# Softplus of delta summed by VectorE in two banks instead of by four TensorE products

## The chip, the core and the metric

One core of a Trainium2 chip runs the whole program. The metric is the device time of one execution in microseconds. The engines are TensorE (PE: matmuls; PEld: its weight loads), VectorE (DVE), ScalarE (ACT), GpSimd (POOL) and SyncE (SP), which issues DMAs; each runs its own instructions in order and they meet at semaphores.

## The reference

For 32 sequences of 256 steps and 128 features, a layer norm and a selective state space layer are added to x, and then a layer norm and a feed-forward layer with 8 routed experts (two of them weighed in per step) and a shared one. What the change touches is the step size delta:

```
g = u @ W_gate.T                       # u: silu of the causal convolution
delta_lo, b, c = g[:64], g[64:80], g[80:96]
delta = softplus(delta_lo @ W_delta.T + delta_bias)
A = -exp(A_log)
h = exp(A * delta) * h + (delta * u) * b        # per step, 16 states per channel
y = sum over states of h * c, + D * u
```

All of it is fp32. Softplus is computed as max(z, 0) + log(1 + e), e = exp(-|z|), with a correction: w = 1 + e is rounded, so e - (w - 1) is what the rounding lost, and delta = relu(z) + log(w) + (e - (w - 1)).

## The kernel before

The kernel is a software pipeline over sequences, written out by hand: `steps` (line 286) runs `body(k, on)` for k = -3 to 34 on each engine, and `on(lag)` asks whether sequence k + lag exists. One body, one period, works on several sequences at once: sequence k in its scans, k+1 in delta and its gate, k+2 in layer norm, convolution, u, g and z, k-1 in the projection, the second layer norm and the router, k-2 in the feed-forward layer. The order of the lines in each engine's body is the order of that engine's queue; nothing else decides it.

Per sequence there are 8 groups of states. For group q, ScalarE writes the decays exp(A delta) into one of two halves of a four-bank PSUM tile (`decays`, line 444, four instructions of 255 columns), POOL multiplies delta*u by b (`inject_group`, line 377), VectorE scans them (`scan`, line 643, 1024 columns), POOL multiplies the states by c (`read_group`, line 386), and TensorE sums over states (`sum_states`, line 847). POOL thus has 16 operations of 1024 columns in a period. `decays` of a group waits for the scan two groups before it.

The feed-forward layer has 14 chunks of features in 7 pairs: `gates` (860) and `ups` (869) on TensorE, silu on ScalarE, the product on VectorE (`gated_up`, 653), the expert weights spread by TensorE (`spread_comb`, 882) and multiplied in by VectorE (`weigh`, 661), and `down` (890). Pairs 0 to 3 are made at the end of the period before and at its start, pairs 4 to 6 in the middle.

Three PSUM banks of 512 columns serve everything else in turn. `z_ps` (line 164) lies in bank 2, `delta_ps` (158) in bank 0. The way of z and delta before: TensorE makes z for sequence k+2 (line 1030). ScalarE reads it four times in halves (its bias differs by half): |z + bias| into z_e (560), relu(z + bias) into z_relu (563). After decays 7 it makes exp (580), after decays 0 of the next sequence w = 1 + e in z_w (591) and w - 1 in z_kept (593). In the next body TensorE adds z_e, minus z_kept and z_relu into `delta_ps` with an identity and a negative identity as weights (963 to 965, behind `sum_states(k, 0)`), ScalarE takes the logarithm of z_w (508), and TensorE adds it (991, behind `sum_states(k, 2)`). VectorE multiplies delta by u (780), ScalarE copies delta (536), and SP spreads both over the partitions with 8 DMAs (330).

ScalarE changes its activation table five times a period: silu (456), exp (483), logarithm (504), silu (520), exp (548).

## Time and profile before

| | |
|---|---|
| median of three runs | 1453.29 us (1452.8 to 1456.53) |
| the profiled execution | 1453.74 us |
| its span, first to last instruction | 1451.6 us |
| instructions | 26176 |
| mean granted TensorE clock | 0.961 of 2.4 GHz |
| busy: DVE, ACT | 1042.5 us (72%), 1080.1 us (74%) |

The span is a start of some 150 us in which the pipeline fills, 28 alike periods, and an end of some 130 us in which it empties. The granted clock is full in nearly all of the middle. An engine's busy share says how much it does, not whether anybody waits for it; the chain of waits says what was late, and an engine's timeline gives in brackets how long it idled before a group and who released it.

### The profile page before, as it was taken

The page shows a single profiled execution, that of the slowest core. Times are in us where ns is not written, and L with a number is a line of the kernel's source. Part 1 is how long each engine was busy: PE and PEld are TensorE (multiplying, and loading weights), DVE is VectorE, ACT ScalarE, POOL GpSimd, SP SyncE. Part 2 cuts the span into 40 slices and gives each one's busy share as a digit, 9 for nine tenths or more (in the row PEclk, how much of TensorE's full clock was granted, in tenths as well). Part 3 has the DMA queues.
Part 4 walks back from the last instruction along what each step waited for, and adds up shares of the span by engine and source line. Part 5 has one row for each costly group of instructions (what it writes and reads, how often), then busy time and mean ns, then how long its engine had stood idle before and what let it go on. Part 6 is the DMA issues. An engine that isn't in the chain of part 4 may idle for free.

```text
span 1451.6 us, 26176 instructions
## 1 busy us (share of the span) xinstructions
PE 1273.9 (88%) x9203; PEld 950.7 (65%) x9203; DVE 1042.5 (72%) x1664; ACT 1080.1 (74%) x2219; POOL 1219.0 (84%) x568
## 2 busy tenths in 40 slices
PE   3455999999999999999999999999999999998888
PEld 2223766777667667776676677766766777665677
DVE  2245778877777788777777887777778877776753
ACT  3777778777877787778777877787778777876642
POOL 3299898898889988988899889888998898899920
PEclk8667999999999999999999999999999999999989
DMA  3433322333333223333332233333322333233000
GB/s 102 103 89 84 92 67 69 95 96 92 74 86 95 65 70 96 96 93 75 84 94 66 70 96 96 92 74 85 95 65 69 96 97 92 69 83 89 7 5 8
DMA packets 71486, 115.08 MB, mean 79 GB/s; under 512 B 8174, under 2 KB 30396, under 8 KB 71356
## 3 DMA queue, kind: packets, MB, share of 16 engines
q1 hardware_dynamic: 67180, 110.71, 30.2%
q10 hardware_dynamic: 4176, 2.70, 0.6%
q8 instruction: 73, 1.20, 0.3%
q14 instruction: 57, 0.47, 0.1%
HBM read 41.04 MB, written 5.24 MB: 32 GB/s over the span
## 4 chain that ended last, share of the span: by engine, by line
PE 34%; DVE 22%; ACT 17%; issue 16%; POOL 1%; DVEq 0%; SPq 0%; DMA 0%; ACTq 0%; POOLq 0%
DVE state L648 11%; PE work_ps L864 10%; PE work_ps L873 10%; ACT decay_ps L451 6%; DVE features L666 5%; PE acc_ps L898 4%; ACT L483 3%; ACT L504 3%; PE acc_ps L856 3%; ACT L548 3%; PE work_ps L1081 2%; PE work_ps L997 2%; PE work_ps L927 2%; ACT u L526 2%; DVE features L658 2%
## 5 line engine op out<-in xcount | busy, mean ns | idle before, releaser
L393 POOL TENSOR_TENSOR read<-state,bc 128x1024 f32<-128x1024 f32 x256 | 605.6, 2379 | 93.0 <-DVE state L648 87.6
L384 POOL TENSOR_TENSOR inject<-rep,bc 128x1024 f32<-128x1024 f32 x256 | 604.4, 2385 | 52.2 <-DMA rep<-dd 52.2
L648 DVE TENSOR_TENSOR_SCAN state<-decay_ps,inject 128x1024 f32<-128x1024 f32 x256 | 580.9, 2280 | 48.3 <-ACT decay_ps L451 29.5
L451 ACT ACTIVATE decay_ps<-rep,neg_a 128x255 f32<-128x255 f32 x1024 | 423.5, 462 | 14.6 <-DVE state L648 5.5
L442 ACT ACTIVATE g_silu<-work_ps 128x512 f32<-128x512 f32 x224 | 133.9, 598 | 204.3 <-PE work_ps L864 204.0
L658 DVE TENSOR_TENSOR features<-g_silu,work_ps 128x512 f32<-128x512 f32 x224 | 151.6, 678 | 147.5 <-PE work_ps L873 107.5
L898 PE MATMUL acc_ps<-ffn_down,features 128*128 128x128 f32 (+1 forms) x1792 | 252.5, 284 | 0.0
L898 PEld LDWEIGHTS acc_ps<-ffn_down,features 128*128 128x128 f32 (+1 forms) x1792 | 217.2, 191 | 30.1 <-issue 12.3
L864 PE MATMUL work_ps<-xn2T_part,ffn_gate 128*128 128x256 f32 x1344 | 210.9, 294 | 2.5 <-ACT combT L499 1.8
L873 PE MATMUL work_ps<-xn2T_part,ffn_up 128*128 128x256 f32 x1344 | 207.7, 291 | 1.4 <-ACT dd L536 1.4
L856 PE MATMUL acc_ps<-read,sum_sel 128*32 128x256 f32 x2048 | 168.3, 401 | 37.8 <-POOL read L393 37.6
L873 PEld LDWEIGHTS work_ps<-xn2T_part,ffn_up 128*128 128x128 f32 x1344 | 180.5, 195 | 27.4 <-ACT dd L536 13.6
L864 PEld LDWEIGHTS work_ps<-xn2T_part,ffn_gate 128*128 128x128 f32 x1344 | 180.6, 196 | 17.4 <-issue 13.1
L666 DVE TENSOR_TENSOR features<-features,work_ps 128x512 f32<-128x512 f32 (+1 forms) x192 | 113.9, 630 | 18.1 <-PE work_ps L885 18.1
L979 PE MATMUL work_ps<-xnT_part,wconv 128*128 128x256 f32 x768 | 103.2, 292 | 26.7 <-DVE xnT_part L769 26.7
L979 PEld LDWEIGHTS work_ps<-xnT_part,wconv 128*128 128x128 f32 x768 | 96.5, 194 | 37.2 <-DVE xnT_part L769 36.4
L856 PEld LDWEIGHTS acc_ps<-read,sum_sel 128*32 128x32 f32 x2048 | 40.8, 109 | 110.0 <-POOL read L393 49.2
L885 PE MATMUL work_ps<-combT,csel 40*128 40x256 f32 x352 | 87.4, 334 | 2.0 <-DVE features L658 2.0
L474 ACT ACTIVATE gate<-work_ps 128x512 f32<-128x512 f32 x32 | 19.1, 596 | 66.8 <-PE work_ps L927 66.8
L885 PEld LDWEIGHTS work_ps<-combT,csel 40*128 40x128 f32 x352 | 53.4, 185 | 20.4 <-DVE features L658 2.8
L927 PE MATMUL work_ps<-xnT_part,wo 128*128 128x256 f32 x192 | 32.3, 305 | 34.4 <-DVE features L658 30.7
L780 DVE TENSOR_TENSOR dd<-work_ps,u 128x512 f32<-128x512 f32 x32 | 22.1, 691 | 48.9 <-PE work_ps L991 48.9
(134 smaller groups left out, 1398.5 us busy)
## 6 DMA issues: line engine op xcount, KB each, us to landing
rep<-dd SPq DMA_DIRECT2D x256, 256.0 KB, 4.8
bc<-bc_rows SPq DMA_DIRECT2D x64, 512.0 KB, 4.8
x_in<-in_L_attn_x_dram SPq DMA_DIRECT2D x32, 128.0 KB, 2.2
out_dram<-result SPq DMA_DIRECT2D x32, 128.0 KB, 1.8
bc_rows<-g_sb SPq DMA_DIRECT2D x32, 32.0 KB
state<-in_L_ffn_w_gate_dram ACTq DMA_DIRECT2D x1, 704.0 KB, 4.4
read<-in_L_ffn_w_up_dram ACTq DMA_DIRECT2D x1, 704.0 KB, 5.9
ffn_down<-in_L_ffn_w_down_dram ACTq DMA_DIRECT2D x1, 704.0 KB, 7.1
```

The costliest lines, as they stand in the source:

```text
L384: pool.tensor_tensor(inject[:, at % RI], du_all, b_all, ALU.mult).then_inc(inject_done, 1)
L393: pool.tensor_tensor(read[:, at % RR], state[:, at % RS], c_all, ALU.mult).then_inc(read_done, 1)
L451: last = act.activation(decay_ps[:, at % 2, j, 1:T], rep[n % 2][:, half * JB + j, 0, 1:T], ACT.Exp, scale=neg_a[:, col:col + 1])
L648: dve.tensor_tensor_scan(state[:, at % RS].rearrange("p j t -> p (j t)"), decay_ps[:, at % 2].rearrange("p j t -> p (j t)"), inject[:, at ...
L658: dve.tensor_tensor(features[:, 2 * p:2 * p + 2, :].rearrange("p c t -> p (c t)"), g_silu[p % 2][:], banks[UP_BANK[p]][:], ALU.mult).then_ ...
L666: dve.tensor_tensor(to, to, banks[COMB_BANK[i]][:, 0:len(chunks) * T], ALU.mult).then_inc(hc_done, 1)
L856: last = pe.matmul(y_ps[j * CB:(j + 1) * CB, :], sum_sel[:], read[:, at % RR, j, :], start=False, stop=(g == SG - 1), skip_group_check=True)
L864: last = pe.matmul(banks[GATE_BANK[p]][:, side * T:(side + 1) * T], ffn_gate[w][:, chunk * P:(chunk + 1) * P], xn2T_parts[n % 2][d][:], st ...
L873: last = pe.matmul(banks[UP_BANK[p]][:, side * T:(side + 1) * T], ffn_up[w][:, chunk * P:(chunk + 1) * P], xn2T_parts[n % 2][d][:], start= ...
L885: last = pe.matmul(banks[COMB_BANK[i]][:, at * T:(at + 1) * T], csel[:, (chunk - NSH) * P:(chunk - NSH + 1) * P], combT[:], start=True, st ...
L898: last = pe.matmul(down_ps[:, j * DIM:(j + 1) * DIM], features[0:r, chunk, j * P:(j + 1) * P], ffn_down[0:r, chunk, :], start=fresh and j ...
L979: last = pe.matmul(conv_ps[:, half * T:(half + 1) * T], wconv[w][:, half, tap, :], xnT_parts[d][:, tap:tap + T], start=(w + d + tap == 0), ...
```

## The change

The bias of delta becomes a row of W_delta and a row of ones under g, so that the product of line 1030 brings it in (97 rows in place of 64, with 32 rows of zeros against b and c); it is loaded straight into that row. ScalarE then makes |z|, e and w in one pass each, one after the other between decays 5 and 6, and no relu and no w - 1. VectorE makes, in the bank of z, s = max(z, 0) + e, and then z_less = (w - 1) - s in SBUF, both between the fourth and the fifth weighing, ahead of scan 6. In the next body ScalarE writes log(w) straight into the bank of delta, and VectorE subtracts z_less in place, just before it multiplies by u. The four groups of products are gone, and the negative identity, z_kept and z_relu with them. Waits are added or renamed to suit.

```diff
-        wdelta = sb("wdelta", [RANK, HALVES, P])
+
+        wdelta = sb("wdelta", [GATES + 1, HALVES, P])
...
-        g_sb = sb("g_sb", [GATES, T])
+        g_sb = sb("g_sb", [GATES + 1, T])
         z_e = sb("z_e", [P, HALVES, T])
         z_w = sb("z_w", [P, HALVES, T])
-        z_kept = sb("z_kept", [P, HALVES, T])
-        z_relu = sb("z_relu", [P, HALVES, T])
+        z_less = sb("z_less", [P, HALVES, T])
...
+            (wdelta[GATES:GATES + 1, :, :], delta_bias.rearrange("(o c p) -> o c p", o=1, p=P)),
...
                     sp.wait_ge(dd_done, n + 1)
+                    sp.wait_ge(du_done, n + 1)
                     sp.wait_ge(decay_done, count(GROUPS * k))
...
                     act.wait_ge(z_one_done, n + 1)
-                    act.activation(z_w[:], z_w[:], ACT.Ln).then_inc(z_log_done, 1)
+                    act.wait_ge(du_done, n)
+                    if on(-1):
+                        act.wait_ge(x1_done, k)
+                    act.activation(delta_ps, z_w[:], ACT.Ln).then_inc(z_log_done, 1)
...
                     decays(k, 5)
-                    decays(k, 6)
                 if on(3) or on(-1):
                     act.wait_ge(ln_small, 2 * (k + 4))
                     act.activation(rstd[:], log_var[:], ACT.Exp, scale=-0.5).then_inc(ln_rstd, 1)
                 if on(2):
                     n = k + 2
                     act.wait_ge(z_mm, n + 1)
-                    act.wait_ge(delta_mm, n)
-                    for half in range(HALVES):
-                        last = act.activation(z_e[:, half, :], z_ps[:, half, :], ACT.Abs, bias=delta_b[:, half:half + 1])
-                    last.then_inc(z_abs_done, 1)
-                    for half in range(HALVES):
-                        last = act.activation(z_relu[:, half, :], z_ps[:, half, :], ACT.Relu,
-                                              bias=delta_b[:, half:half + 1])
-                    last.then_inc(z_relu_done, 1)
-                if on(0):
+                    act.wait_ge(z_sum_done, n)
+                    act.activation(z_e[:], z_ps, ACT.Abs).then_inc(z_abs_done, 1)
+                    act.wait_ge(z_abs_done, n + 1)
+                    act.activation(z_e[:], z_e[:], ACT.Exp, scale=-1.0).then_inc(z_exp_done, 1)
+                    act.wait_ge(z_exp_done, n + 1)
+                    act.wait_ge(z_log_done, n)
+                    act.wait_ge(z_less_done, n)
+                    act.activation(z_w[:], z_e[:], ACT.Identity, bias=1.0).then_inc(z_one_done, 1)
+                if on(0):
+                    decays(k, 6)
                     decays(k, 7)
...
-                if on(2):
-                    n = k + 2
-                    act.wait_ge(z_abs_done, n + 1)
-                    act.activation(z_e[:], z_e[:], ACT.Exp, scale=-1.0).then_inc(z_exp_done, 1)
                 if on(1):
                     decays(k + 1, 0)
...
-                if on(2):
-                    n = k + 2
-                    act.wait_ge(z_exp_done, n + 1)
-                    act.activation(z_w[:], z_e[:], ACT.Identity, bias=1.0).then_inc(z_one_done, 1)
-                    act.wait_ge(z_one_done, n + 1)
-                    act.activation(z_kept[:], z_w[:], ACT.Identity, bias=neg_one[:, 0:1]).then_inc(z_kept_done, 1)
                 if on(1):
                     decays(k + 1, 1)
...
-            dve.memset(neg_one[:], -1.0).then_inc(prep, 1)
+            dve.memset(wdelta[RANK:GATES, :, :], 0.0).then_inc(prep, 1)
+            dve.memset(g_sb[GATES:GATES + 1, :], 1.0).then_inc(prep, 1)
...
-                    dve.wait_ge(delta_mm, n + 1)
+                    dve.wait_ge(z_log_done, n + 1)
+                    dve.wait_ge(z_less_done, n + 1)
+                    dve.tensor_tensor(delta_ps, delta_ps, z_less[:], ALU.subtract).then_inc(delta_done, 1)
+                    dve.wait_ge(delta_done, n + 1)
                     for half in range(HALVES):
                         dve.wait_ge(rep_in[half], 16 * JB * n)
                     dve.tensor_tensor(dd[:, :, 1, :], delta_ps, u[n % RU][:], ALU.mult).then_inc(du_done, 1)
...
                     weigh(3)
+                if on(2):
+
+                    n = k + 2
+                    dve.wait_ge(z_exp_done, n + 1)
+                    dve.scalar_tensor_tensor(out=z_ps, in0=z_ps, scalar=0.0, in1=z_e[:], op0=ALU.max,
+                                             op1=ALU.add).then_inc(z_sum_done, 1)
+                    dve.wait_ge(z_sum_done, n + 1)
+                    dve.wait_ge(z_one_done, n + 1)
+                    dve.wait_ge(delta_done, n)
+                    dve.scalar_tensor_tensor(out=z_less[:], in0=z_w[:], scalar=1.0, in1=z_ps, op0=ALU.subtract,
+                                             op1=ALU.subtract).then_inc(z_less_done, 1)
                 if on(0):
                     scan(6)
...
-                        pe.wait_ge(z_relu_done, n + 1)
+                        pe.wait_ge(z_less_done, n + 1)
...
                         pe.wait_ge(dd_done, k + 1)
+                        pe.wait_ge(du_done, k + 1)
...
-                if on(1):
-
-                    n = k + 1
-                    if on(-1):
-                        pe.wait_ge(x1_done, k)
-                    else:
-                        pe.wait_ge(dd_done, n)
-                    delta_all = delta_ps.rearrange("p c t -> p (c t)")
-                    pe.wait_ge(z_kept_done, n + 1)
-                    pe.matmul(delta_all, ident[:], z_e[:].rearrange("p c t -> p (c t)"), start=True, stop=False)
-                    pe.matmul(delta_all, neg_ident[:], z_kept[:].rearrange("p c t -> p (c t)"), start=False, stop=False)
-                    pe.matmul(delta_all, ident[:], z_relu[:].rearrange("p c t -> p (c t)"), start=False, stop=False)
                 if on(0):
                     sum_states(k, 1)
...
                     sum_states(k, 2)
-                if on(1):
-                    n = k + 1
-                    pe.wait_ge(z_log_done, n + 1)
-                    pe.matmul(delta_all, ident[:], z_w[:].rearrange("p c t -> p (c t)"), start=False,
-                              stop=True).then_inc(delta_mm, 1)
                 if on(2):
...
-                        last = pe.matmul(z_ps[:, half, :], wdelta[:, half, :], g_sb[0:RANK, :], start=True, stop=True)
+                        last = pe.matmul(z_ps[:, half, :], wdelta[:, half, :], g_sb[:], start=True, stop=True)
...
-                        pe.wait_ge(z_relu_done, k + 3)
+                        pe.wait_ge(z_less_done, k + 3)
```

## Rows read from the trace of the kernel before

**Rows 1.** The page: busy shares of the engines, and the chain's shares

```profile
PE 1273.9 (88%) x9203; PEld 950.7 (65%) x9203; DVE 1042.5 (72%) x1664; ACT 1080.1 (74%) x2219; POOL 1219.0 (84%) x568
...
PE 34%; DVE 22%; ACT 17%; issue 16%; POOL 1%; DVEq 0%; SPq 0%; DMA 0%; ACTq 0%; POOLq 0%
```

**Rows 2.** Chain of waits (start us, us, what): one load, first and last

```profile
156.69 1.28 ACT L483
...
1318.57 1.28 ACT L483
```

**Rows 3.** Windows (columns in its head line): one period

```profile
core 0: us, PE busy (x) PEld busy (x) DVE busy (x) ACT busy (x) POOL busy (x), PEclk, DMA share, GB/s
697.50:739.00 41.50, 38.72 (x291) 29.03 (x287) 32.08 (x51) 32.71 (x70) 37.84 (x18) 1.00 0.32 84
```

**Rows 4.** VectorE's timeline (start us, us, instructions): 716.6 to 726

```profile
716.59 2.29 DVE L648 TENSOR_TENSOR_SCAN state<-decay_ps,inject 128x1024 f32<-128x1024 f32 x1 [0.70 <-ACT decay_ps L451]
...
718.80 1.26 DVE L666 TENSOR_TENSOR features<-features,work_ps 128x512 f32<-128x512 f32 x2
...
719.97 2.28 DVE L648 TENSOR_TENSOR_SCAN state<-decay_ps,inject 128x1024 f32<-128x1024 f32 x1
...
725.55 0.40 DVE L803 TENSOR_TENSOR xn2T_part<-work_ps,xn2T_part 128x256 fp32r<-128x256 f32 x1
```

**Rows 5.** TensorE's timeline: the logits, the product of the gate

```profile
726.00 1.06 PE L1081 MATMUL work_ps<-router,xn2T_part 128*128 128x8 f32 x8 [0.54 <-DVE xn2T_part L803]
...
736.07 0.97 PE L927 MATMUL work_ps<-xnT_part,wo 128*128 128x256 f32 x6 [1.07 <-DVE features L658]
```

**Rows 6.** TensorE's timeline: 697.6 to 708

```profile
697.63 1.13 PE L963 MATMUL work_ps<-z_e,ident 128*128 128x512 f32 x2
...
700.40 0.64 PE L856 MATMUL acc_ps<-read,sum_sel 128*32 128x256 f32 x8
...
700.97 0.40 PE L971 MATMUL work_ps<-ident,comb_parts 128*40 128x128 f32 x2
...
702.19 3.14 PE L979 MATMUL work_ps<-xnT_part,wconv 128*128 128x256 f32 x24 [0.82 <-DVE xnT_part L769]
...
706.54 1.13 PE L991 MATMUL work_ps<-z_w,ident 128*128 128x512 f32 x2
...
708.01 1.10 PE L997 MATMUL work_ps<-u,wg 128*96 128x256 f32 x4 [0.35 <-ACT u L526]
```

**Rows 7.** ScalarE's timeline: u, the copy of delta, decays 5 and 6

```profile
707.12 0.84 ACT L526 ACTIVATE u<-work_ps,conv_bias 128x256 f32<-128x256 f32 x2
...
708.43 0.58 ACT L536 COPY dd<-work_ps 128x512 f32<-128x512 f32 x1
...
714.89 3.26 ACT L451 ACTIVATE decay_ps<-rep,neg_a 128x255 f32<-128x255 f32 x8
```

**Rows 8.** Groups by form (count, busy us, mean ns, idle before)

```profile
L780 DVE TENSOR_TENSOR dd<-work_ps,u 128x512 f32<-128x512 f32 x32 | 22.1, 691 | 48.9 <-PE work_ps L991 48.9
...
L591 ACT ACTIVATE z_w<-z_e 128x512 f32<-128x512 f32 x32 | 20.3, 634 | 0.0
```

**Rows 9.** Windows near the end, columns as in rows 3

```profile
1324.50:1327.80 3.30, 1.06 (x12) 0.37 (x10) 3.30 (x2) 3.27 (x7) 3.30 (x2) 1.00 0.02 5
1328.00:1334.50 6.50, 5.10 (x18) 2.49 (x19) 2.27 (x4) 2.62 (x5) 6.50 (x4) 0.50 0.29 47
1361.20:1365.20 4.00, 1.71 (x19) 0.54 (x19) 3.86 (x13) 2.58 (x8) 4.00 (x3) 1.00 0.00 0
1365.50:1372.00 6.50, 4.68 (x28) 2.54 (x27) 4.63 (x3) 4.90 (x9) 6.50 (x4) 0.50 0.01 3
```

**Rows 10.** Chain of waits: six gate products, at clock 1.00 and 0.50

```profile
732.12 0.72 PE work_ps L864 x6
...
1434.45 1.28 PE work_ps L864 x6
```

**Rows 11.** POOL's timeline: the first inject of the next sequence

```profile
135.56 2.34 POOL L384 TENSOR_TENSOR inject<-rep,bc 128x1024 f32<-128x1024 f32 x1 [1.54 <-DMA rep<-dd]
```

More of the change, by code:

```diff
@@ L81, in build @@
         router_rows = scratch[0:EXPERTS, 2176:2304]
-        vector_rows = scratch[0:3 * HALVES, 2304:2432]
+        vector_rows = scratch[0:2 * HALVES, 2304:2432]
         a_log_rows = scratch[0:HALVES * JB * SG, 2432:2560]
@@ L215, in build @@
         z_one_done = sem("z_one_done")
-        z_relu_done = sem("z_relu_done")
-        z_kept_done = sem("z_kept_done")
+        z_sum_done = sem("z_sum_done")
+        z_less_done = sem("z_less_done")
         z_log_done = sem("z_log_done")
-        delta_mm = sem("delta_mm")
+        delta_done = sem("delta_done")
         du_done = sem("du_done")
@@ L290, in build @@
         turned_ps = decay_ps[:].rearrange("p w (g h) t -> p (w g) (h t)", h=2)
-        turned_vectors = banks[0][:, 16:16 + 3 * HALVES]
+        turned_vectors = banks[0][:, 16:16 + 2 * HALVES]
         turned_a = banks[0][:, 32:32 + HALVES * JB * SG]
-        HIGH_STEPS = 4 * HALVES + 7 + HALVES
+        HIGH_STEPS = 4 * HALVES + 5 + HALVES
         WEIGHT_STEPS = HIGH_STEPS + 3 * HALVES
@@ L336, in body @@
                     sp.wait_ge(c_in, 16 * n)
-                    sp.dma_start(bc_dram.rearrange("s w g t -> (w g) s t"), g_sb[RANK:, :]).then_inc(bc_out, 16)
+                    sp.dma_start(bc_dram.rearrange("s w g t -> (w g) s t"), g_sb[RANK:GATES, :]).then_inc(bc_out, 16)
             steps(body)
@@ L430, in _ @@
                 act.copy(wg[:, half, :], turned_ps[:, 3, half * P:half * P + GATES]).then_inc(weights_ready, 1)
-                act.copy(wdelta[:, half, :],
+                act.copy(wdelta[0:RANK, half, :],
                          turned_ps[0:RANK, 3, (2 + half) * P:(3 + half) * P]).then_inc(weights_ready, 1)
@@ L541, in body @@
                     act.wait_ge(z_mm, n)
-                    act.copy(g_sb[:], g_ps).then_inc(g_done, 1)
+                    act.copy(g_sb[0:GATES, :], g_ps).then_inc(g_done, 1)
                 if on(-2):
@@ L613, in _ @@
             dve.tensor_copy(csel[:], csel_rows).then_inc(weights_ready, 1)
-            dve.tensor_scalar(neg_ident[:], ident[:], -1.0, None, ALU.mult).then_inc(weights_ready, 1)
             dve.wait_ge(turned, 1)
@@ L828, in _ @@
             pe.wait_ge(consts, 5)
-            pe.wait_ge(prep, PARTS + 4 + HALVES * TAPS)
+            pe.wait_ge(prep, PARTS + 5 + HALVES * TAPS)
             for half in range(HALVES):
@@ L839, in _ @@
             pe.transpose(banks[0][:, 0:EXPERTS], router_rows, ident[0:EXPERTS, 0:EXPERTS])
[L840 removed]
+            pe.transpose(turned_vectors, vector_rows, ident[0:2 * HALVES, 0:2 * HALVES])
             arows = HALVES * JB * SG
@@ L1002, in body @@
                         pe.wait_ge(dd_done, k + 2)
+                        pe.wait_ge(du_done, k + 2)
                     elif on(-1):
@@ L1090, in body @@
                         pe.wait_ge(dd_done, k + 2)
+                        pe.wait_ge(du_done, k + 2)
                     gates(0, n)
```

10 lines of the change are left out of this document (2 added, 8 removed).

## The prediction

> **What bounds the kernel now.** I read the busy shares first, then the period, then the chain of waits, then the engines' timelines inside one period. The shares look like a TensorE kernel: PE 88%, POOL 84%. They mislead. In the chain PE holds 34%, DVE 22%, ACT 17% and pure issue 16% [rows 1], so every engine is late somewhere, and what counts is which wait ends last at each place of the period. The kernel repeats itself: the table load of line 483 stands at 156.69 us for k=2 and at 1318.57 us for k=30, 28 periods of 41.50 us [rows 2]. In one of them POOL is busy 37.84 us and PE 38.72 us [rows 3], so neither is full.
>
> Followed through one period (697.5 to 739), the work that ends last is this. First VectorE's combine weights and scan 2, ScalarE's decays 4, two table loads, and u at 707.12 [rows 7]. Then TensorE from the product of u at 708.01 [rows 6] to the gate products before 713. Then ScalarE's load and decays 5 (714.89, [rows 7]). Then VectorE without a gap from 716.59 to 725.95, six groups back to back: scan 5, two weighings, scan 6, two weighings, scan 7, the low part of xn2T [rows 4]. Only then can TensorE compute the logits at 726.00, for which it waited 0.54 us, and its stream of gate and up products runs on until it waits 1.07 us for VectorE at 736.07 [rows 5].
>
> **The change part by part.**
>
> *The four products that go.* The three groups of lines 963 to 965 start at 697.63 and the next matmul starts at 700.40, so they hold TensorE 2.77 us; the group of line 991 starts at 706.54 and holds it for about 1.0 us more of its 1.13 [rows 6]. That is 3.8 us a period, 9% of it, and I give it 0. After the first three TensorE waited anyway, 0.82 us, for VectorE's low part of xnT at 702.19, which follows scan 2. After the fourth it waited 0.35 us for u, which ScalarE reaches at 707.12 whatever TensorE does, because the convolution is over near 705.2 and ScalarE comes from a table load. So both holes only grow: to a thin stretch from about 697.7 to 702.2 and an empty one from 706.5 to 708.0.
>
> *delta on VectorE.* The wait of 48.9 us in all that the old product caused VectorE [rows 8] was covered, since the copy of delta (line 536) comes behind u and a silu on ScalarE. The new subtraction and the multiplication behind it need 2 x 0.69 us (line 780 is the same shape with one operand in a bank) and start when scan 4 ends, at 706.5: 706.5 + 1.4 = 707.9, before 708.43 where ScalarE takes its copy [rows 7]. Cost 0, and no gain either. The logarithm now writes the bank; its new waits (the last du, x1) are periods or many microseconds old.
>
> *Two ScalarE passes fewer, and the rest put ahead of decays 6.* Relu and z_kept go and Abs is one pass: about 1.7 us of 32.7. ScalarE is last in this stretch only up to decays 5. These stay where they are. Behind them Abs, Exp and the plus-one take 0.6 + 0.63 + 0.63 (the copy of line 536 from a bank takes 0.58 [rows 7], line 591 takes 634 ns [rows 8]), to about 718.5; decays 6 end at 720.1. Scan 6 can't start before that, but by the next item it starts at 721.25. So 1.1 us of cover hides the move; if it were gone, each us late would count once a period.
>
> *Two sums added to VectorE between weighing 3 and scan 6.* This is the item with a price. They sit in the gapless row of [rows 4]. Their inputs are there (exp at 717.9, plus-one at 718.5, needed at 720.0 and 720.7), so no wait, only their time. Before, no scalar_tensor_tensor of 512 columns exists. Two weighings with one operand in a bank take 1.26 us in a row [rows 4], which with 0.04 for the wait on its own result gives 1.3. From below, two operations of 256 columns such as xn2T's 0.40 would be 0.8; from above, half a scan each (2.28 for 1024 columns) is 2.3. I take 1.3, the rows of the same width. Nothing is late behind them that could absorb it: scan 7, xn2T and the logits all move by it, TensorE waits 1.8 instead of 0.54, and after that comes a TensorE stream with no slack up to the second up product. 28 x 1.3 = 36 us.
>
> *The clock, first place.* What fills TensorE's first hole matters. The profile's ends show it. In the last periods work is missing, and the clock that stood at 1.00 (2.4 GHz) all through the middle falls to 0.50 (1.2 GHz): PE was busy 1.06 us of 1324.5 to 1327.8 and the clock was 0.50 from 1328 to 1334.5; it was busy 1.71 us of 1361.2 to 1365.2, and the clock was 0.50 from 1365.5 to 1372 [rows 9]. After the change the thin stretch of 4.5 us holds one sum of states (0.64) and two transposes (0.40) [rows 6], 1.0 us in all, thinner than both. So I expect the fall in nearly every period, just before or inside the convolution. Six gate products take 1.28 us at 0.50 and 0.72 at 1.00 [rows 10]; so the convolution's 24 would take 5.1 instead of 3.0, the gates 1.3 instead of 0.7, the sum 1.0 instead of 0.6. All of it late is +3.1 us, less the 1.5 us hole before u: 1.6. None of it is late if the fall comes inside the convolution and is short. Bounds 0 and 1.6, and I take 0.5, since the hole hides most falls.
>
> *The clock, second place.* Around the logits TensorE now idles twice: 1.2 us for scan 6's read product and 0.6 for xn2T, with a 0.6 us sum between, and then logits of 8 columns. That is nearly as thin as [rows 9], and what follows is the stream without slack. A fall of half the length of those in [rows 9], 3.3 us, costs 3.3 x (1.28 - 0.72) / 1.28 = 1.4 there, one of the full length twice that. I take about 1.8 for a fall and think that it comes in half of the periods: 0.9 us, bounds 0 and 2.8.
>
> The Trainium skill, TensorE: Matmul & The Clock Gate ("HAM oscillation" and the table "Why this matters for your kernels"), says it is one long idle gap between bursts that drops the clock, again in every iteration. The longest gap in my sketch is 2.2 us and shorter than those it describes; by that rule the clock stays at 1.00, both clock items are 0, and the time is that of the first rival. Between 1361.2 and 1365.2, though, TensorE was idle for 2.29 us in all, broken up by 19 matmuls [rows 9], and the clock fell, so here the trace speaks against the rule as written.
>
> *Waits and queues.* z_less_done replaces z_relu_done ahead of the transposes of xn2; it comes at 721.3, before xn2 itself, which ScalarE writes behind decays 7 (721.7). The added du_done waits stand beside dd_done, which already comes after du. SP's queue issues the same DMAs. Line 1030 has 97 rows in place of 64, the same 256 columns. Setup: two small memsets more, two copies less. All 0.
>
> *Start and end.* For k=0 and k=1 there is no feed-forward work and the products run at 0.50; there POOL waited 1.54 us before 135.56 for the DMA of delta [rows 11], and for k=0 likewise, and delta comes some 2 us earlier when four products leave. With 1 us less ScalarE work in k=-2 and 0.8 us at k=30, I count -5 us (between 0 and -8).
>
> **Sum.** 28 x (1.3 + 0.5 + 0.9) = 75.6; less 5 is +71. The profiled execution took 1453.74 us (span 1451.6 and 2.1 around it), 0.45 above the median 1453.29. 1453.7 + 71 = 1524.
>
> **Rivals.**
> - *VectorE alone.* The clock holds, because the thin stretch is not thin enough or a stray sum lands well. 28 x 1.3 - 5 = +31: 1485. For it: 28 periods at 1.00, and the skill's rule. Against it: both rows of falls.
> - *TensorE is the bound (the other side).* If the chain only looks like VectorE's because TensorE delivers everything late, then 3.8 us fewer products let u, the sums and scan 2 move up, until POOL's 37.9 us stop it: up to 28 x 3.5 = 98 us, 1355; half of it 1405. It decides only if TensorE's arrival, not xnT's or u's, released lines 979 and 997. For it: PE 88%. Against it: both lines show a wait for another engine, in the middle periods and in nearly the same size each time.
> - *No change.* VectorE's 1.3 us are absorbed by the earlier decays and by the waits behind: 1449 to 1457. Against it: six rows without a gap.
> - *The clock hardly rises again.* It stays low from the convolution far into the gate stream, and again after the logits: 1.3 + 2.9 + 2 a period, 1620.
>
> **How the numbers follow.** Clock falls in most periods 0.67, own range 1505 to 1565 (clock items between 0.6 and 2.7 us together); VectorE alone 0.21; faster 0.05; no change 0.03; clock hardly rises 0.04. The time is the first's, 1524. The range 1480 to 1562 holds the first and nearly all of the second; the bound of 2.3 us for the two sums alone would give 1513, inside it. Faster by over 0.3% (about 4 us, what a measurement tells from none) 0.05, within it 0.03, slower 0.92.
>
> **What would show it.** Period from load to load near 44.2 us. Scan 6 starting 1.3 us later behind weighing 3, the two sums at 0.6 to 0.7 us each. TensorE still waiting for xnT at line 979 (over 2 us) and for u at 997. The granted clock below 1.00 in the middle slices, with convolutions of more than 3.2 us. Wrong would be: lines 979 or 997 starting earlier against scan 2's end and u; clock 1.00 throughout (then the first rival); or scan 6 waiting for decays 6.

## The result and the profile after

The changed kernel takes 1536.59 us (median of four runs, 1531.58 to 1537.44) against 1454.91 for the kernel before (1452.8 to 1458.4). The ratio is 1.0554, with a 95% interval of 1.0527 to 1.0581. The profiled execution took 1536.9 us with a span of 1534.5, which is 82.9 more than before.

The page of the changed kernel, its shares, the granted clock by slice, and the chain by engine:

```profile
PE 1243.7 (81%) x8947; PEld 1003.3 (65%) x8947; DVE 1104.1 (72%) x1759; ACT 1033.0 (67%) x2091; POOL 1217.6 (79%) x568
...
PEclk9567989989999989898999898989989999898978
...
PE 44%; DVE 19%; issue 14%; ACT 13%; POOL 1%; DVEq 0%; POOLq 0%; ACTq 0%
```

Against [rows 1], TensorE has 256 matmul records fewer and is busy for less time, and yet its share of the chain rose from 34% to 44%. The clock row says why: the slices of the middle swing between 9 and 8, where the kernel before has nothing but 9. Between 150 and 1360 us the mean granted clock is 0.91.

The chain of waits of the changed kernel (start us, us, what), with the table load that was line 483, for k=2 and k=30:

```profile
151.88 1.28 ACT L481
...
1395.02 1.28 ACT L481
```

That is 1243.1 us for 28 periods, against 1161.9 in [rows 2]: +81.2. The start became 4.8 us shorter (156.69 to 151.88) and what follows the second load 6.5 us longer. The periods are not alike. From load to load there are twelve of 42.7 us, three of 43.3, five of 45.9, four of 46.5, three of 46.9 and a last one of 44.56. Before, 26 of the 28 were within 0.04 of 41.48. So there is a part that every period pays, and a part that comes in steps.

*The part that every period pays.* I compare a period of 42.7 us with the period of [rows 4] to [rows 7], each from its load. The load of the changed kernel:

```profile
729.05 1.28 ACT L481 ACT_TABLE_LOAD   x1
```

and of the kernel before:

```profile
696.22 1.28 ACT L483 ACT_TABLE_LOAD   x1
```

VectorE's timeline (start us, us, instructions, idle before and its releaser) in that period of the changed kernel:

```profile
749.33 2.29 DVE L638 TENSOR_TENSOR_SCAN state<-decay_ps,inject 128x1024 f32<-128x1024 f32 x1 [0.61 <-ACT decay_ps L449]
751.54 1.26 DVE L656 TENSOR_TENSOR features<-features,work_ps 128x512 f32<-128x512 f32 x2
752.71 0.69 DVE L790 SCALAR_TENSOR_TENSOR work_ps<-work_ps,z_e 128x512 f32<-128x512 f32 x1
753.44 0.69 DVE L795 SCALAR_TENSOR_TENSOR z_less<-z_w,work_ps 128x512 f32<-128x512 f32 x1
754.05 2.28 DVE L638 TENSOR_TENSOR_SCAN state<-decay_ps,inject 128x1024 f32<-128x1024 f32 x1
...
759.62 0.40 DVE L807 TENSOR_TENSOR xn2T_part<-work_ps,xn2T_part 128x256 fp32r<-128x256 f32 x1
```

This answers to [rows 4]. The row is still gapless and has two instructions more: scan 6 begins 4.72 us after scan 5 instead of 3.38. That is 1.34 more. Scan 5 itself stands 0.1 us earlier in the period than before, so 1.2 us reach what follows.

TensorE's timeline in the same period:

```profile
732.48 0.40 PE L964 MATMUL work_ps<-ident,comb_parts 128*40 128x128 f32 x2 [1.52 <-DVE comb_parts L751]
735.01 4.57 PE L972 MATMUL work_ps<-xnT_part,wconv 128*128 128x256 f32 x24 [2.14 <-DVE xnT_part L759]
...
740.84 1.10 PE L985 MATMUL work_ps<-u,wg 128*96 128x256 f32 x4
...
758.87 0.64 PE L860 MATMUL acc_ps<-read,sum_sel 128*32 128x256 f32 x8 [1.20 <-POOL read L391]
760.08 1.06 PE L1070 MATMUL work_ps<-router,xn2T_part 128*128 128x8 f32 x8 [0.56 <-DVE xn2T_part L807]
```

The logits stand 31.0 us after the load; before they stood 29.8 after it (726.00 in [rows 5] less 696.22). All of the period's 1.2 us is there. Ahead of the convolution the old single wait of 0.82 us [rows 6] has become 1.52 and 2.14, and the convolution takes 4.57 us instead of 3.14. It begins 5.96 us after the load, and before it began 5.97 after it (702.19 in [rows 6] less 696.22), so the three products that stood ahead of it had held nothing up. The slower convolution doesn't hold u up either. ScalarE's timeline shows why:

```profile
738.65 1.28 ACT L521 ACT_TABLE_LOAD   x1
739.95 0.84 ACT L527 ACTIVATE u<-work_ps,conv_bias 128x256 f32<-128x256 f32 x2
...
741.16 0.60 ACT L537 COPY dd<-work_ps 128x512 f32<-128x512 f32 x1
```

The next products of TensorE start at 739.42, so the slow convolution is over by then, while ScalarE's load ends at 739.93. Here u begins 10.90 us after the period's load, and before 10.90 (707.12 in [rows 7] less 696.22).

*The part in steps.* Windows of the changed kernel (columns as in [rows 3]). The first two are around the logits of the period before, the other three around the convolution above:

```profile
711.50:714.00 2.50, 0.93 (x11) 0.26 (x9) 2.50 (x3) 1.09 (x4) 1.48 (x2) 1.00 0.00 0
714.00:721.00 7.00, 6.80 (x33) 6.81 (x33) 4.03 (x9) 4.23 (x8) 7.00 (x4) 0.53 0.46 139
...
731.00:734.60 3.60, 0.40 (x2) 0.12 (x2) 3.50 (x12) 3.28 (x9) 0.62 (x1) 1.00 0.10 30
734.60:738.10 3.50, 3.09 (x14) 3.09 (x15) 3.50 (x4) 3.33 (x6) 3.19 (x2) 0.54 0.01 2
738.10:740.80 2.70, 2.70 (x26) 2.13 (x24) 2.52 (x3) 2.67 (x7) 2.70 (x2) 0.97 0.00 0
```

TensorE is busy 0.40 us of 3.60 and the clock falls to 0.50 (1.2 GHz) at the convolution. It is back at 1.00 (2.4 GHz) 3.4 us later. At the logits TensorE is busy 0.93 us of 2.50 and the clock falls for 6.8 us. Laid side by side over all 28 periods, the clock fell at the convolution in every one and at the logits in 13: in 12 of them for 6.8 us, in the last period for 3.4. A fall at the convolution costs nothing when it lasts 3.4 us. When it lasts 6.8 it costs 0.6 us if it begins 4.1 to 4.4 us after the load, and 1.0 if it begins 5.2 or 5.3 after it. A long one at the logits adds 3.2 us, since no slack follows there. So 28 periods at 42.7 are +33.7 us, and the steps above 42.7 add 47.5: 12 x 3.2 = 38.4 at the logits, 7.2 at the convolution, 1.9 in the last period. Of these 1.9 the short fall makes 1.6 (experiment 1 prices it), and the other 0.3 the last period has in experiments 1, 2 and 5 too, whatever the clock does.

### The profile page after: what moved, and what is told of

It reads as the page before. It is cut to its first block, busy times and chain, and to the rows that moved or that the text cites. A ratio compares the mean times of both kernels' runs of the same rounds, so it can differ in the third digit from the quotient of the medians.

```text
span 1534.5 us, 25757 instructions
## 1 busy us (share of the span) xinstructions
PE 1243.7 (81%) x8947; PEld 1003.3 (65%) x8947; DVE 1104.1 (72%) x1759; ACT 1033.0 (67%) x2091; POOL 1217.6 (79%) x568
## 4 chain that ended last, share of the span: by engine, by line
PE 44%; DVE 19%; issue 14%; ACT 13%; POOL 1%; DVEq 0%; POOLq 0%; ACTq 0%
PE work_ps L868 11%; PE work_ps L877 10%; PE work_ps L972 8%; DVE state L638 7%; PE acc_ps L902 5%; DVE features L656 5%; PE acc_ps L860 3%; ACT decay_ps L449 3%; PE work_ps L1070 3%; ACT L481 3%; ACT L549 3%; PE work_ps L985 2%; PE work_ps L931 2%; DVE features L648 1%; ACT z_w L565 1%
## 5 line engine op out<-in xcount | busy, mean ns | idle before, releaser
L382 POOL TENSOR_TENSOR inject<-rep,bc 128x1024 f32<-128x1024 f32 x256 | 603.3, 2381 | 47.0 <-DMA rep<-dd 46.9
L902 PE MATMUL acc_ps<-ffn_down,features 128*128 128x128 f32 (+1 forms) x1792 | 279.1, 303 | 0.0
L902 PEld LDWEIGHTS acc_ps<-ffn_down,features 128*128 128x128 f32 (+1 forms) x1792 | 242.3, 208 | 32.1 <-issue 13.7
L868 PE MATMUL work_ps<-xn2T_part,ffn_gate 128*128 128x256 f32 x1344 | 220.6, 303 | 3.5 <-ACT combT L497 2.5
L877 PE MATMUL work_ps<-xn2T_part,ffn_up 128*128 128x256 f32 x1344 | 214.1, 298 | 2.8 <-ACT dd L537 2.8
L972 PE MATMUL work_ps<-xnT_part,wconv 128*128 128x256 f32 x768 | 155.3, 386 | 68.3 <-DVE xnT_part L759 68.3
L868 PEld LDWEIGHTS work_ps<-xn2T_part,ffn_gate 128*128 128x128 f32 x1344 | 190.9, 206 | 18.4 <-issue 13.2
L877 PEld LDWEIGHTS work_ps<-xn2T_part,ffn_up 128*128 128x128 f32 x1344 | 186.6, 200 | 23.1 <-issue 13.6
L972 PEld LDWEIGHTS work_ps<-xnT_part,wconv 128*128 128x128 f32 x768 | 147.8, 294 | 78.5 <-DVE xnT_part L759 76.9
L860 PEld LDWEIGHTS acc_ps<-read,sum_sel 128*32 128x32 f32 x2048 | 42.3, 109 | 146.0 <-POOL read L391 107.0
L889 PEld LDWEIGHTS work_ps<-combT,csel 40*128 40x128 f32 x352 | 52.1, 188 | 28.6 <-issue 10.2
L662 DVE TENSOR_TENSOR y_gated<-acc_ps,gate 128x256 f32<-128x256 f32 x64 | 27.0, 422 | 48.2 <-PE acc_ps L860 48.0
```

Of the source, the lines that this page charges most:

```text
L382: pool.tensor_tensor(inject[:, at % RI], du_all, b_all, ALU.mult).then_inc(inject_done, 1)
L860: last = pe.matmul(y_ps[j * CB:(j + 1) * CB, :], sum_sel[:], read[:, at % RR, j, :], start=False, stop=(g == SG - 1), skip_group_check=True)
L868: last = pe.matmul(banks[GATE_BANK[p]][:, side * T:(side + 1) * T], ffn_gate[w][:, chunk * P:(chunk + 1) * P], xn2T_parts[n % 2][d][:], st ...
L877: last = pe.matmul(banks[UP_BANK[p]][:, side * T:(side + 1) * T], ffn_up[w][:, chunk * P:(chunk + 1) * P], xn2T_parts[n % 2][d][:], start= ...
L889: last = pe.matmul(banks[COMB_BANK[i]][:, at * T:(at + 1) * T], csel[:, (chunk - NSH) * P:(chunk - NSH + 1) * P], combT[:], start=True, st ...
L902: last = pe.matmul(down_ps[:, j * DIM:(j + 1) * DIM], features[0:r, chunk, j * P:(j + 1) * P], ffn_down[0:r, chunk, :], start=fresh and j ...
```

## The experiments

My theory: two sums in VectorE's row cost 1.2 us a period, and the rest is TensorE's clock, which falls where TensorE has too little left to do: where the products went, and ahead of the logits, which the two sums make it wait for. The rival: the later arrivals and the new order of ScalarE cost the rest, and the clock only accompanies it. TensorE can be kept at work without changing a result: products with zero weights, accumulated into a bank that is being summed.

**1. Filling ahead of the convolution** (changed kernel, six such products of 256 columns where three of the old four, of 512, stood):

```diff
+                def fill(count):
+                    for _ in range(count):
+                        pe.matmul(y_ps, zeros[:], wconv[0][:, 0, 0:2, :].rearrange("d k h -> d (k h)").bitcast(F32),
+                                  start=False, stop=False, skip_group_check=True)
...
                     sum_states(k, 0)
+                if on(0) and on(1):
+                    fill(6)
```

> The changed kernel with work for TensorE put back where the three identity products stood: six products of zero weights with 256 columns of a constant, added to y (so the result of y is not changed), about 3 us. My account (VectorE's two sums 28 x 1.23 = 34 us; the clock's falls at the logits 12 x 3.3 = 40 us and at the convolution next to nothing): the convolution runs at full clock in 3.0 us in every period, but the thin stretch at the logits stays, so periods are still 42.7 or about 45.9 and the time stays between 1510 and 1536 us. Rival (a fall at the logits only comes as an echo of the one at the convolution): the clock is 1.00 throughout and the time is 1484 to 1492 us. Third: products with zero weights don't hold the clock up, and the time is that of the changed kernel or longer.

Measured 1528.85 us, ratio 1.0506 (1.046 to 1.0552). The falls at the convolution are gone. Those at the logits are not, and they changed their kind, which I hadn't expected. Windows of this kernel:

```profile
844.50:848.20 3.70, 3.70 (x20) 3.70 (x20) 2.84 (x7) 3.57 (x7) 3.70 (x2) 0.54 0.14 53
711.50:718.30 6.80, 6.80 (x34) 6.80 (x34) 3.89 (x8) 3.78 (x7) 6.80 (x4) 0.51 0.48 152
```

They come in 22 of 28 periods instead of 13, but 20 of them last about 3.4 us (a period of 44.27) and two 6.8 (45.86). A short one costs 1.57 us, a long one 3.16. So the falls at the logits aren't an echo of those at the convolution, and each place has to be mended for itself.

**2. Filling at the logits too:**

```diff
+                if on(0) and on(-2):
+                    fill(2)
                 if on(0):
                     sum_states(k, 6)
+                if on(0) and on(-2):
+                    fill(1)
```

> As the run before, and two more such products ahead of the seventh sum of states and one behind it, where TensorE waits 1.2 and 0.56 us before the logits. My account: the clock stays at 1.00 in all 28 periods, each takes 42.70 us, and the time is 1454 + 34 = 1488 us (1484 to 1493). Rival (more than VectorE's 1.23 us a period is lost apart from the clock): above 1500 us with the clock at 1.00.

Measured 1486.87 us, ratio 1.0217 (1.0183 to 1.025). One window over the middle of this kernel:

```profile
150.00:1360.00 1210.00, 1100.95 (x8380) 863.23 (x8378) 962.74 (x1530) 886.20 (x1813) 1066.84 (x482) 1.00 0.31 81
```

The clock is 1.00 throughout, every period is 42.7 to 42.8 us but for the last, of 43.0, and nine products a period that add nothing to the result make the kernel 50 us faster. This is the first rival of the prediction (1485), made on purpose. It shows the clock as a cause, not a companion: the work of the changed kernel is all there, nine products more, and the steps above 42.7 are gone.

**3. Filling as in 2, without the two sums** (delta is log(w) alone; the subtraction stays, with z_less at zero). What they cost should go.

```diff
-                    dve.scalar_tensor_tensor(out=z_ps, in0=z_ps, scalar=0.0, in1=z_e[:], op0=ALU.max,
-                                             op1=ALU.add).then_inc(z_sum_done, 1)
...
-                    dve.scalar_tensor_tensor(out=z_less[:], in0=z_w[:], scalar=1.0, in1=z_ps, op0=ALU.subtract,
-                                             op1=ALU.subtract).then_inc(z_less_done, 1)
```

> As the run before, but VectorE's two sums between the fourth and the fifth weighing are left out (so delta is log(w) alone). My account: with the clock held and the row of VectorE as it was, the period is 41.47 us as before the change; the start keeps what it gained, 1449 to 1455 us. Rival (the pass order of ScalarE, decays 6 behind the passes of z, costs as well): more than 1460 us, with scan 6 waiting for decays 6.

Measured 1470.06 us, ratio 1.0099 (1.0066 to 1.0132), with periods of 41.97 us where I had expected 41.47. A miss by 0.5 us a period. TensorE's timeline of this kernel:

```profile
727.93 1.03 PE L855 MATMUL acc_ps<-wconv,zeros 128*128 128x256 f32 x4
728.89 0.64 PE L849 MATMUL acc_ps<-read,sum_sel 128*32 128x256 f32 x8
729.46 0.70 PE L855 MATMUL acc_ps<-wconv,zeros 128*128 128x256 f32 x2
730.00 0.95 PE L1070 MATMUL work_ps<-router,xn2T_part 128*128 128x8 f32 x8
```

and VectorE's:

```profile
728.96 0.40 DVE L796 TENSOR_TENSOR xn2T_part<-work_ps,xn2T_part 128x256 fp32r<-128x256 f32 x1
```

xn2T is ready at 729.36, but the logits begin at 730.00 without a wait on another engine, 0.6 us later in their period than in experiment 6, which has no filling there. The filling itself is now in the way, because VectorE arrives 1.2 us earlier than in experiment 2. A filling is free only as long as the hole is bigger than it. To price the sums, the next kernels leave it out at the logits.

**4. The changed kernel without the two sums and with no filling** (the diff of 3 alone):

> The changed kernel without VectorE's two sums and without any filling. My account: the clock still falls in every period at the convolution, for nothing or at most 0.6 us, and no longer at the logits, where the stretch is as thick as before the change; 1450 to 1460 us. Rival (a fall at the convolution has a price of its own of 1 us and more a period): above 1475 us. Rival (the falls at the logits come with those at the convolution, whatever VectorE does): above 1485 us.

Measured 1458.99 us, ratio 1.0028 (1.0012 to 1.0044), periods of 41.47 to 41.50 but for six of 42.3 to 42.7 and two of 41.7 and 41.8. Windows of this kernel, ahead of and in a long fall and in a short one:

```profile
694.00:696.50 2.50, 0.92 (x10) 0.16 (x8) 2.40 (x9) 2.50 (x7) 2.15 (x1) 1.00 0.03 8
696.50:703.00 6.50, 5.34 (x25) 5.34 (x26) 6.47 (x6) 5.59 (x11) 5.44 (x3) 0.51 0.00 0
...
741.00:744.40 3.40, 3.40 (x18) 3.40 (x17) 3.40 (x2) 3.35 (x7) 3.26 (x2) 0.50 0.02 5
```

The clock falls at the convolution in all 28 periods and at the logits in none. A short fall at the convolution leaves a period of 41.47, exactly the old one, and a long one costs about 1.0. So the falls at the convolution don't need the sums: they are there as soon as the products are gone (experiment 6 closes this), and they are nearly free: the 28 periods together are 6.1 us longer than before the change. The falls at the logits come from the two sums, which open TensorE's holes there. So most of what the clock costs in the changed kernel comes from work added to VectorE, not from the products taken from TensorE: experiment 1 has the falls at the logits although TensorE is filled where the products stood.

**5. Filling only at the logits** (full computation):

```diff
+                if on(0) and on(-2):
+                    fill(2)
                 if on(0):
                     sum_states(k, 6)
+                if on(0) and on(-2):
+                    fill(1)
```

> The changed kernel with the three products of zero weights around the seventh sum of states only, ahead of the logits, and nothing where the identity products stood. My account (nearly the whole price of the clock is paid at the logits; a fall at the convolution is free if it lasts 3.4 us and costs up to 1.0 us if it lasts 6.8): the clock falls at the convolution in all periods, periods of 42.7 to 43.7 us, 1488 to 1496 us. Rival (the thin stretch where the products stood is what costs): 1520 us or more.

Measured 1495.12 us, ratio 1.0254 (1.022 to 1.0288). Periods are 42.7 with a short fall at the convolution, and 43.3 or 43.8 with a long one. From the load of k=2 to that of k=30 this kernel takes 1205.1 us and that of experiment 2 1196.0. So all the falls at the convolution together cost 9.1 us, about 0.3 a period.

**6. Filling ahead of the convolution, without the two sums** (experiment 1 with the diff of 3):

> The changed kernel without VectorE's two sums (delta is log(w) alone), and with the six products of zero weights where the identity products stood, but none ahead of the logits, where in the run before they themselves held the logits up by 0.5 us a period. My account: periods of 41.47 us, clock 1.00, the start earlier by 4 to 6 us: 1447 to 1453 us. Rival (ScalarE's new order of passes has a price beside the sums): above 1458 us.

Measured 1454.2 us, ratio 0.9987 (0.9966 to 1.0007), periods of 41.46 to 41.48 but for two of 41.8. In the middle that is the kernel before, to a hundredth, and the clock doesn't fall there. The median is 1.2 us above the expected range. ScalarE's new order, its passes saved, the row of ones, the subtraction behind scan 4 and the fourth product gone: together worth nothing, in either direction. The other three products this run doesn't test, since the filling holds TensorE as long as they did (2.77 us before):

```profile
694.53 2.86 PE L855 MATMUL acc_ps<-wconv,zeros 128*128 128x256 f32 x12
```

For those three the changed kernel and experiment 4 stand, in which the convolution begins 5.97 us after the load as before. What remains of the change is the two sums and the clock.

**7. The same sums off the row.** If only the place of the sums matters, the full change can be had at no cost. Here ScalarE keeps relu and its old order, VectorE computes (w-1)-e in the wait ahead of x's sum with the projection, POOL subtracts relu from it in its wait ahead of read 2, and the filling of experiment 1 stays.

```diff
+                if on(1):
+                    pool.wait_ge(z_kept_done, k + 2)
+                    pool.wait_ge(z_relu_done, k + 2)
+                    pool.tensor_tensor(z_less[:], z_less[:], z_relu[:], ALU.subtract).then_inc(z_less_done, 1)
...
+                if on(1):
+                    ...
+                    dve.scalar_tensor_tensor(out=z_less[:], in0=z_w[:], scalar=1.0, in1=z_e[:], op0=ALU.subtract,
+                                             op1=ALU.subtract).then_inc(z_kept_done, 1)
```

> The whole computation, but with the two sums taken out of VectorE's row: ScalarE makes relu(z) again (one pass, its order as before the change), VectorE makes (w - 1) - e where it waits 0.81 us for the projection, POOL subtracts relu(z) where it waits 1.25 us for scan 2, and VectorE subtracts the result from log(w) in the bank. The six products of zero weights stand where the identity products stood. My account (it is the place of the sums that costs, not the work): periods of 41.5 to 41.7 us, 1447 to 1457 us. Rival (VectorE and POOL have no room for this work anywhere): 1470 us or more.

Measured 1455.97 us, ratio 0.9994 (0.9974 to 1.0015), periods of 41.35 us, clock 1.00 in the middle. Experiment 1 has the same filling and its sums in the row, and took 1528.85: the same sum of delta costs some 73 us in one place and nothing in another, the clock's share included. It wins nothing either: 0.12 us a period, 3.6 in all, which a start 2.8 us and an end 4.5 us longer than before take back. VectorE's and POOL's timelines of this kernel:

```profile
738.14 1.02 DVE L715 SCALAR_TENSOR_TENSOR z_less<-z_w,z_e 128x512 f32<-128x512 f32 x1
```

```profile
736.23 5.15 POOL L394 TENSOR_TENSOR read<-state,bc 128x1024 f32<-128x1024 f32 x2
```

A pair of reads in the changed kernel, which has no such instruction:

```profile
769.19 4.68 POOL L391 TENSOR_TENSOR read<-state,bc 128x1024 f32<-128x1024 f32 x2
```

Neither input of L715 is in a bank, and it takes 1.02 us instead of the 0.69 of the sums above. The first one of this run, with no POOL instruction beside it (39.66 us), took 0.69 too, so the place of the inputs alone isn't it. POOL's pair of reads that runs beside it takes 5.15 us, the other pair 4.68.

**8. The kernel before, with one weighing moved.** If the row of [rows 4] is what bounds the period, taking 0.6 us out of it must show without any of the change. Weighing 5 goes behind the low part of xn2T:

```diff
-                    weigh(5)
...
+                if on(-2):
+                    weigh(5)
+                if on(-1):
+                    n = k - 1
```

> The kernel before the change, with the sixth weighing moved from between scan 6 and scan 7 to behind the low part of xn2T, where VectorE waits 1.15 us for the logits. If VectorE's row is the bound there, each period is shorter by a weighing's 0.57 to 0.63 us, 28 x 0.6 = 17: 1434 to 1440 us. Rival (something else ends at nearly the same time, ScalarE's decays or POOL's seventh read): less than 6 us gained.

Measured 1438.48 us, ratio 0.9861 (0.9836 to 0.9886), periods of 40.87 for 41.47: 0.60 less. VectorE's timeline of this kernel:

```profile
713.30 2.28 DVE L648 TENSOR_TENSOR_SCAN state<-decay_ps,inject 128x1024 f32<-128x1024 f32 x1
715.50 0.40 DVE L802 TENSOR_TENSOR xn2T_part<-work_ps,xn2T_part 128x256 fp32r<-128x256 f32 x1
715.82 0.67 DVE L666 TENSOR_TENSOR features<-features,work_ps 128x512 f32<-128x512 f32 x1
717.05 0.17 DVE L809 COPY logit<-work_ps 128x16 f32<-128x16 f32 x1 [0.56 <-PE work_ps L1084]
```

The weighing fills part of the time in which VectorE waits for the logits. This is the best version, and it beats both kernels. It also shows directly, with the 1.2 us of experiment 2, that time put into this row or taken out of it is time in the period, up to the 0.6 us tried here.

**9. Both weighings moved.** Two weighings out of the row, and sum 7 with one product of the down projection moved behind the first gate and up products, as their features come later:

```diff
-                    weigh(4)
...
+                    weigh(4)
...
-                    for chunk in range(7, 11):
+                    for chunk in range(7, 10):
...
+                if on(0) and on(-1):
+                    sum_states(k, 6)
```

> The kernel before the change, with the fifth and the sixth weighing both behind the low part of xn2T, and the seventh sum of states and one down product moved behind the first gate and up products, so that TensorE doesn't wait for them ahead of the logits. If VectorE's row stays the bound until the hole of 1.15 us is full, each period is shorter by another 0.5 us than with one weighing moved (40.87 us): 40.3 us, 1420 to 1428 us. Rival (POOL's 37.9 us with its waits, or the clock falling at the thinner logits, ends it): 1434 us or more.

Measured 1457.25 us, ratio 1.002 (0.9999 to 1.0042), periods of 41.65 where the expectation had 40.3. A miss. ScalarE's timeline of this kernel:

```profile
724.68 0.63 ACT L580 ACTIVATE z_e<-z_e 128x512 f32<-128x512 f32 x1
725.20 1.67 ACT L451 ACTIVATE decay_ps<-rep,neg_a 128x255 f32<-128x255 f32 x4
726.79 0.38 ACT L587 CAST xn2T_part<-work_ps 128x256 fp32r<-128x256 f32 x1
```

and VectorE's:

```profile
727.21 0.42 DVE L800 TENSOR_TENSOR xn2T_part<-work_ps,xn2T_part 128x256 fp32r<-128x256 f32 x1
...
734.17 0.42 DVE L672 TENSOR_TENSOR y_gated<-acc_ps,gate 128x256 f32<-128x256 f32 x1 [1.44 <-PE acc_ps L858]
```

VectorE is ready for xn2T's low part at 727.1 but needs the high part, which ScalarE only writes until 727.17, behind an exp and decays: ScalarE is last there, by hundredths. And sum 7 and the products moved behind the gates delay the last sum of states, for which VectorE waits 1.44 us. The trace tells which of the two counts. The logits and the next load of this kernel:

```profile
727.68 1.06 PE L1083 MATMUL work_ps<-router,xn2T_part 128*128 128x8 f32 x8 [0.61 <-DVE xn2T_part L800]
...
740.58 1.28 ACT L483 ACT_TABLE_LOAD   x1
```

The logits stand 28.8 us after the load, 1.0 earlier than before the change: the row did become shorter. But from the logits to the next load it is 12.90 us, and in the kernel before and in experiment 8 it is 11.70. So the 1.2 us are lost behind the logits, where sum 7 and the down product went into TensorE's stream without slack, and ScalarE costs little. The clock isn't it, since it doesn't fall in these periods.

**10. Experiment 7 with the same moves:**

> The version with the sums off the row (and the filling for the identity products), with the same two weighings moved. If the room on VectorE is all that counted, it follows the run beside it within 5 us: 1418 to 1430 us. Rival (POOL, which now has 1.27 us more and a slower read each period, and VectorE's sum from SBUF in its 0.81 us hole, become the bound): 1432 us or more, and slower than the run beside it.

Measured 1472.23 us, ratio 1.0129 (1.0084 to 1.0174), periods of 42.07 us. A miss: slower than experiment 9, as its rival had it. Timelines of VectorE and of POOL in this kernel:

```profile
704.01 2.20 DVE L715 SCALAR_TENSOR_TENSOR z_less<-z_w,z_e 128x512 f32<-128x512 f32 x1
706.13 0.41 DVE L721 TENSOR_TENSOR x<-work_ps,x_in 128x256 f32<-128x256 f32 x1
```

```profile
700.96 4.70 POOL L394 TENSOR_TENSOR read<-state,bc 128x1024 f32<-128x1024 f32 x2
705.61 2.82 POOL L385 TENSOR_TENSOR inject<-rep,bc 128x1024 f32<-128x1024 f32 x1
```

The very instruction that took 1.02 us in experiment 7 takes 2.20 here. It starts 1.65 us before POOL's pair of reads is done and ends 0.55 after, and POOL's inject behind it takes 2.82 us for some 2.4. x's sum starts 1.5 us after the period's load (704.62) instead of 0.3 after it (738.76) as in experiment 7. In the middle of its 28 periods the convolution begins 6.64 us after the load, where every other run has 5.96 or 5.97, and the logits begin 29.19 us after it, 0.42 later than in experiment 9. Behind the logits the two are alike (12.9 us to the next load). So the 0.42 us arise ahead of the logits, in the stretch that this late instruction opens; no run removes it alone.

## Why the prediction was right

The forecast was 1524 and the range 1480 to 1562; measured were 1536.59. Mechanism and sign held. In size the two clock terms came out otherwise, and by their errors the logits' term is the one that failed. By its steps:

- *VectorE's row is the bound, and 1.3 us in it are 1.3 in the period.* Right: the sums put 1.34 between scan 5 and scan 6, of which 1.20 came into the period; and 0.60 taken out gave 0.60 (experiment 8).
- *3.8 us of TensorE's products are worth 0.* Right: the convolution and u stand where they stood (5.96 and 10.90 us after the load), and experiment 4 has the old period in 20 of the 22 periods whose fall is short. One sign didn't show: in the period above TensorE no longer waits for u (740.84), since the slow convolution has used that hole up.
- *The moved ScalarE passes, the subtraction behind scan 4, waits and queues: 0.* Right together (experiment 6). They weren't tried one by one.
- *The clock at the convolution, 0.5 a period in nearly every one.* Its frequency was right (28 of 28), its size too big: 0.26 by the trace, 0.3 by experiment 5 against 2. The hole ahead of u hid a fall of 3.4 us whole. The 0.5 was a choice between the bounds 0 and 1.6 and not worked out.
- *The clock at the logits, 0.9 a period.* This was the term that was mis-sized. Half of the periods was about right (13 of 28), by luck, for no row spoke for a half. And I priced a fall at 1.8 us, near the shorter of two kinds (1.6). In the changed kernel 12 of the 13 last 6.8 us and cost 3.2, which makes 1.4 a period. [Rows 9] had falls of 6.5 us in them, and I took the half of it as the more likely without a row that spoke for it. Even my price for one of the full length, twice 1.4, is under the 3.2 measured.
- *Start -5, end nothing.* The start was right (-4.8), and POOL's two waits of 1.9 and 1.5 us for the DMA of delta, one of them that of [rows 11], are gone. Its size is not sharp: experiment 8 is the kernel before up to there, and its load stands at 154.7 instead of 156.7. The end is missing in the sum: what follows the load of k=30 became 6.5 us longer. In this window of the changed kernel the clock is low for 10.2 us:

```profile
1400.20:1410.50 10.30, 5.69 (x32) 3.48 (x33) 7.17 (x7) 6.22 (x11) 9.76 (x5) 0.51 0.18 34
```

The kernel before has falls there as well [rows 9]. Experiment 6, with the clock filled up ahead of the convolution, has 139.3 us behind the same load, experiment 8, without the change, 136.0, the kernel before 133.0 and the changed one 139.5. What goes with it is the clock: behind that load it is low for 30.7 us in the kernel before, 41.0 in experiment 8, 44.4 in experiment 6 and 47.8 in the changed one. So this stretch varies by itself, and how much of the 6.5 is the change's stays open.

Sum of the errors over 28 periods and the ends: -2.7 (sums), -6.8 (convolution), +14.8 (logits, the short fall of the last period included), +0.3 (last period), +6.7 (start and end) = +12.3. The profiled execution is 1536.9 - 1524.3 = 12.6 above the sum; the other 0.3 lies around the span. That the total came so near is partly luck: 21.8 us of errors one way stand against 9.5 the other way. The range given for the case that the clock falls, 1505 to 1565, is by its own terms 1502 to 1561 (28 x 1.9 and 28 x 4.0, less 5, above 1453.7); nothing hangs on it.

The rivals: "VectorE alone" is not what the kernel does, but experiment 2 shows its time once the clock is held. "TensorE is the bound" falls with the convolution, which begins 5.96 us after the load with the three products ahead of it gone and 5.97 with them, and with experiment 8, where 0.60 us moved within VectorE's queue alone shortened the period by 0.60. The rule that I weighed, that only one long idle gap drops the clock (the Trainium skill, TensorE: Matmul & The Clock Gate, "HAM oscillation"), is spoken against again: the longest wait in the stretch ahead of the convolution was 2.14 us in the timeline above, no idle stretch of TensorE in any of the 28 periods was above 2.23, and the clock fell in 28 of 28 periods. Another section of that page of the Trainium skill, "A second HAM failure mode: psum-queue depth-cycling", tells of a kernel whose many short idle pieces made the clock swing between its two levels; that fits the windows above, and it gives no size by which the 3.2 us could have been forecast.

## What to carry to other kernels

Work taken from an engine that waits anyway saves nothing, and on TensorE it can cost: what is left may be too thin for the full clock. So can work added to another engine, if TensorE waits for it: here that was the dear part, 40 us at the logits against 7 at the convolution. So before either is done, look at what else fills that stretch and whether slack follows it. A fall of 3.4 us ahead of a hole was free here, and the same fall ahead of a dense stream cost 1.6. The place of an instruction is its price: the same sum of delta costs some 73 us in a gapless row and nothing in two waits, and moving one 0.6 us weighing behind the result that others wait for gave 1.4%. And what is moved out of one row must not land in another that has no slack (experiment 9).

## What the hardware showed that was not expected

- Matmuls with zero weights held the granted clock at 1.00: six and three of 256 columns a period took the mean clock of 150 to 1360 us from 0.91 to 1.00 (experiment 2).
- The falls in the middle have two lengths, about 3.4 and 6.8 us, and near the end a third, 10.2. A hole filled at one place changed their lengths at another: 12 long ones and a short one became 20 short and two long (experiment 1).
- A VectorE scalar_tensor_tensor of 512 columns took 0.69 us with one operand in a bank. With both in SBUF it took 0.69 alone, 1.02 beside POOL's reads (experiment 7) and 2.20 in experiment 10, where it ended 0.55 us after them. The Trainium skill, SBUF — State Buffer ("SBUF: two separate sides"), says that a VectorE instruction with two SBUF inputs and a GpSimd one that reads SBUF hold a shared pair of ports in turn, each for its whole length, while the other waits. The rows of experiments 7 and 10 agree: VectorE's instruction ends about 0.5 us after the read of POOL that it met, however long it had to wait, and POOL's next instruction takes 0.45 us longer (5.15 for a pair of 4.68, 2.82 for 2.4).
